# Attention kernel: each sum of values issued as two halves of the queries, with a score tile between the halves in TensorE's order

## The reference, cut to what matters

```python
qkv = x @ W_qkv + b_qkv                       # x: 16 x 1024 x 256, layer-normalised
q, k, v = jnp.split(qkv, 3, axis=2)           # 16 heads of 16 features
energy = jnp.einsum('bqhe,bkhe->bqhk', q, k)
attn = jax.nn.softmax(energy, axis=-1) / sqrt(E)
out = jnp.einsum('bihv,bvhd->bihd', attn, v)  # the sum of values
return out.reshape(B, N, E) @ W_out + b_out
```

## Time and profile before

| | us |
|---|---|
| time, median of 3 runs (3433.14 to 3438.01) | 3435.56 |
| time of the profiled execution | 3431.27 |
| its span, first to last instruction | 3429.5 |
| TensorE busy in the span | 3255.2 (95%) |
| VectorE busy | 3007.2 (88%) |
| ScalarE busy | 2703.3 (79%) |
| GpSimd busy | 1069.0 (31%) |
| first and last sum of values start at | 387.2 and 3119.8 |

### The profile page before, as it was taken

One profiled execution on the slowest core, in us unless ns is written; L12 is line 12 of the kernel. 1 busy time (PEld: TensorE's weight loads), 2 busy tenths in 40 slices (PEclk: granted clock), 3 DMA queues, 4 the chain that ended last, 5 costly groups with the idle time before them and its releaser, 6 DMA issues. The chain is left out here.

```text
span 3429.5 us, 61061 instructions
## 1 busy us (share of the span) xinstructions
PE 3255.2 (95%) x22618; PEld 1160.2 (34%) x22618; DVE 3007.2 (88%) x4484; ACT 2703.3 (79%) x5325; POOL 1069.0 (31%) x1021
## 2 busy tenths in 40 slices
PE   6998899999999999999999999999999999998997
PEld 4655222323232323232323232323232323224654
DVE  6866889999999999999999999999999998997865
ACT  5841588888888888888888888888888888887840
POOL 2440233333333232323232323232323232123410
PEclk8999799999999999999999999999999999999998
DMA  4336121313131313131313131313131312122336
GB/s 134 99 139 282 46 65 34 81 34 81 35 80 35 80 36 79 36 78 37 78 36 78 37 77 38 77 38 77 38 77 38 77 38 65 39 80 85 99 125 269
DMA packets 180619, 262.27 MB, mean 76 GB/s; under 512 B 92180, under 2 KB 132948, under 8 KB 165988
## 3 DMA queue, kind: packets, MB, share of 16 engines
q1 hardware_dynamic: 177700, 256.28, 26.9%
q10 hardware_dynamic: 2624, 2.10, 0.2%
HBM read 121.91 MB, written 51.38 MB: 51 GB/s over the span
## 5 line engine op out<-in xcount | busy, mean ns | idle before, releaser
L1706 DVE TENSOR_REDUCE attn_part_max<-attn_ps 128x2 f32<-128x1024 f32 x2048 | 2442.4, 1220 | 213.4 <-PE attn_ps L1839 178.2
L1959 ACT ACTIVATE attn_probs<-attn_ps 128x512 f32<-128x512 f32 x4096 | 2161.5, 598 | 366.6 <-PE attn_ps L1852 366.4
L1852 PE MATMUL attn_ps<-attn_q_rows,attn_k_rows 50*128 50x512 f16 x4096 | 1259.3, 384 | 43.2 <-ACT attn_probs L1959 25.2
L1839 PE MATMUL attn_ps<-attn_k_rows,attn_q_rows 48*128 48x512 f16 x4096 | 1130.5, 386 | 18.9 <-DVE attn_part_max L1706 18.2
L1852 PEld LDWEIGHTS attn_ps<-attn_q_rows,attn_k_rows 50*128 50x128 f16 x4096 | 308.0, 94 | 1329.6 <-ACT attn_probs L1959 1206.9
L1866 PE MATMUL attn_ps<-attn_probs,attn_v_even 128*32 128x512 f32 x4096 | 548.2, 607 | 0.0
L1866 PE MATMUL attn_ps<-attn_probs,attn_v_odd 128*32 128x512 f32 x4096 | 545.5, 605 | 0.7 <-ACT attn_probs L1959 0.7
L1596 POOL CAST attn_max_parts<-attn_max_whole 16x128 f16<-16x128 f32 x128 | 35.9, 280 | 1158.9 <-ACT attn_max_whole L1905 1158.8
L1839 PEld LDWEIGHTS attn_ps<-attn_k_rows,attn_q_rows 48*128 48x128 f16 x4096 | 224.3, 94 | 159.1 <-DVE attn_part_max L1706 138.6
L1800 PE MATMUL attn_ps<-attn_shared,attn_w_qk 128*128 128x256 f16 x1536 | 212.9, 276 | 1.3 <-PEq L26 1.3
L1641 POOL TENSOR_TENSOR attn_alpha_t<-attn_alpha_t 128x256 f32<-128x256 f32 x120 | 88.0, 733 | 294.5 <-ACT attn_alpha_t L1936 258.5
(11 more groups left out here) (216 smaller groups left out, 2741.4 us busy)
## 6 DMA issues: line engine op xcount, KB each, us to landing
attn_q_rows<-attn_alpha_t SPq DMA_DIRECT2D x384, 64.0 KB, 2.3
attn_k_rows<-attn_alpha_t SPq DMA_DIRECT2D x384, 64.0 KB, 2.3
ffn_x_back<-in_L_attn_x SPq DMA_DIRECT2D x16, 1024.0 KB, 13.2
after_first_ffn<-ffn_x_back SPq DMA_DIRECT2D x16, 1024.0 KB, 12.2
attn_slot_out<-attn_alpha_t SPq DMA_DIRECT2D x256, 64.0 KB, 2.3
attn_alpha_t<-inverse_denominators SPq DMA_DIRECT2D x32, 512.0 KB
attn_alpha_t<-after_first_ffn SPq DMA_DIRECT2D x16, 1024.0 KB, 9.9
after_attention<-attn_alpha_t SPq DMA_DIRECT2D x16, 1024.0 KB, 4.6
```

The lines of the kernel that those rows point to most:

```text
L1706: dve.tensor_reduce(part_max[:, G % 2, j, :, t, half], pair, AX.X, ALU.max).then_inc(dve_emptied, 1)
L1839: last = pe.matmul(ps[:, bank + e, :], q_rows[rows_e, G % NG, j, t * P:(t + 1) * P], k_rows[rows_e, G % NG, j, half * HALF:(half + 1) * HA ...
L1852: pe.matmul(ps[:, bank, :], k_rows[rows_e, G % NG, h // 2, kt * P:(kt + 1) * P], q_rows[rows_e, G % NG, h // 2, half * HALF:(half + 1) * H ...
L1959: act.activation(probs[:, quad % NQ, h, :], bank_of(s, b0), ACT.Exp, scale=1.0 / (SCALE * SCALE)).then_inc(act_emptied, 1)
```

## The change

A sum is issued as two halves: first the 256 lower queries of the window for all four heads, then the 256 upper ones. The first half stands behind score 1, ahead of the quad's second max pair; the second half stands behind score 2, where the whole sum stood. Both halves carry the wait for score 3 of the quad before. The semaphore that says that a sum is done is raised after the second half. The last sum of the program is issued as two halves in a row.

```diff
-        return ([("max", v) for v in steps[:1]] + [("score", 4 * quad)] + job + [("score", 4 * quad + 1)]
-                + [("max", v) for v in steps[1:]] + [("score", 4 * quad + 2)]
-                + [("sum", quad - 1)] * (quad > 0) + [("score", 4 * quad + 3)])
+        sums = [[("sum", 2 * (quad - 1) + i)] * (quad > 0) for i in range(2)]
+        return ([("max", v) for v in steps[:1]] + [("score", 4 * quad)] + job + [("score", 4 * quad + 1)] + sums[0]
+                + [("max", v) for v in steps[1:]] + [("score", 4 * quad + 2)] + sums[1] + [("score", 4 * quad + 3)])
...
-            def sum_values(b, b0, quad):
+            def sum_values(b, b0, n):
+
+                quad, half = divmod(n, 2)
+                columns = slice(half * 2 * P, (half + 1) * 2 * P)
                 window, kt = divmod(quad, TT)
                 G = window // CHUNKS
                 s = slot_of("score", 4 * quad + 3, b0)
                 wait(pe, act_emptied, b, lambda i: s(i) + 1)
-                if kt == 0:
+                if kt == 0 and half == 0:
...
                 for h in range(GH):
-                    last = pe.matmul(ps[32 * h:32 * h + 32, 7, :], v_ones[G // NG % 2][:, G % NG, kt, h, :], probs[:, quad % NQ, h, :],
-                                     start=(kt == 0), stop=(kt == TT - 1), skip_group_check=True)
-                last.then_inc(pv_done, 1)
+                    last = pe.matmul(ps[32 * h:32 * h + 32, 7, columns], v_ones[G // NG % 2][:, G % NG, kt, h, :], probs[:, quad % NQ, h, columns],
+                                     start=(kt == 0 and half == 0), stop=(kt == TT - 1), skip_group_check=True)
+                if half == 1:
+                    last.then_inc(pv_done, 1)
```

More of the change, by code:

```diff
@@ L1892, in _ @@
             over_batches(pe, body)
-            sum_values(B - 1, B - 1, QB * B - 1)
+            for half in range(2):
+                sum_values(B - 1, B - 1, 2 * (QB * B - 1) + half)
         @block.scalar
```

## The result

The changed kernel takes 3822.6 us (median of 4 runs, 3817.02 to 3824.08) against 3436.35 before (4 runs): 1.1126 times, 95% interval 1.1112 to 1.114. It is slower by 386 us, where 408 was forecast (3843 us).

The account below looks back on a forecast made before the run. It took the loop through ScalarE (2.39 us) to bound quads without a job and TensorE's own work (2.88) those with one; 200 + 208 = 408 us over 3431.3, plus 4 for the median, gave 3843, range 3690 to 3905.

Parts of the forecast that it names:

- The bound: Quads without a job: loop of score 3, exponential, score 2, sum, 2.39 us; with a job TensorE never waits, 2.88.
- The half at 0.57: Each half of the sum on TensorE was to take 0.57 us, two halves 1.14, against 1.00 whole.
- the part that does not shrink: In each half sum, a fixed time of about 0.14 us that does not fall with the columns.
- Quads without a job, +0.37, 200 us: The 540 quads without a job were to go from 2.39 to 2.76 us each, 200 us in all.
- The gate at 1.07: Without a job, the first half waits for score 3's exponential until 1.07 us after score 3 starts, not 0.78.
- Quads with a job, +0.43, 208 us: In 484 quads with a job, score 1 to score 3 was to go from 1.58 to 2.01 us.
- The sum: 200 us without a job plus 208 with one were to add 408 us, giving 3843 us, 1.12 times.
- rival 1: In quads without a job the first half fills TensorE's wait, gate open at 0.78: +0.08 each, 3686 us; 4 in 100.
- What costs nothing: ScalarE, VectorE, window-end copies, job banks, GpSimd and DMA queues were to add no time; last sum +0.14 once.
- The waits of ScalarE and VectorE: ScalarE's waits for scores and VectorE's for max pairs were each to grow by some 400 us.
- Overlap of sets: Within a half, sets of matmuls were to overlap while they drain, as in the whole sum, giving 0.57 us.

Follow-up runs that it names:

- e2: The kernel before with the whole sum, in its old place, taken of the quad two back instead of one back: 3433.28 us, 0.9993 times the kernel before.
- e3: The changed kernel with both halves taken of the quad two back instead of one back: 3652.68 us, 1.0635 times the kernel before.
- e1: The changed kernel with both halves back to back behind score 2, where the whole sum stood: 3440.92 us, 1.0020 times the kernel before.
- e7: The changed kernel with parts of 128 and 384 queries in place of 256 and 256: 3824.29 us, 1.1126 times the kernel before.
- e4: The changed kernel with first half behind score 2, second behind score 3, window-end copy behind score 3's exponential: 3647.17 us, 1.0623 times the kernel before.
- e6: The kernel before with the whole sum moved behind score 1 and the copy ahead of score 2's exponential: 3885.27 us, 1.1302 times the kernel before.

## Why the prediction was right

- **The bound.** The loop score 3, exponential, score 2, sum, at 2.39, holds where VectorE has nothing to reduce (the last quads), and a lag that loosens only the sum's own wait changes nothing (e2). A lag that loosens the first half's wait gives back some 170 us (e3).
- **The half at 0.57.** Traced 0.57. The reasoning from float32 rows of other shapes held. The number was right, but the part that does not shrink was given to the half, and it belongs to the visit (e1, e7): back to back, two halves cost 1.00, not 1.14. That this made no difference is luck of the case: here the halves are always parted. For e1 the prediction's 0.14 a quad would have given 143 us, and it took 6.
- **Quads without a job, +0.37, 200 us.** Traced 2.75, +0.36, which would be 194 us in 540 quads; all of them together grew by 179. The gate at 1.07 and the max pair and score 2 queued behind it are in the timeline. The rest is in quads that were not at 2.39 before or have no max pair. The eleventh quad of each sequence, where VectorE's reciprocal of 0.93 had delayed a max pair, went from 2.66 to 2.75 only (15 quads, 4 us less). The last 13, without max pairs, grew by 2.1 us together (3 us less), and one early quad with a long wait shrank from 9.3 to 3.9 (6 us less). Some 2 us are not placed.
- **Quads with a job, +0.43, 208 us.** Traced +0.41 to +0.42 with a job alone and +0.46 where it carries a transpose, 202 us together. Of the 0.41, 0.23 is the slot of the max pair, which used to run beside scores, and the rest the second entry and exit; in these quads that division is read from the timeline. The quads without max pairs put the max pair at 0.22 where there is no job.
- **The sum.** So 408 forecast, 381 in the quads, 5 outside them. No large errors cancel: both sums are a little high. The recorded range goes down to 3690 and was to take in rival 1, which by its own sum is at 3686; the measured time is far from either.
- **What costs nothing.** No wait of VectorE or of the max pairs' banks became a gate: TensorE's idle time for VectorE ahead of max pairs is 13.5 us, where it was 18.2 before. The copy at a window's end delays the gate by 0.2 in quads without a job, as before. In the 15 quads with a job behind a window's end the kernel before paid it too (3.08), and the changed kernel does not (3.29), which makes these grow by 0.21 only.
- **The step that missed.** The waits of ScalarE and VectorE were to grow by some 400 us each and grew by 278 and 303. Busy time of the exponentials grew from 2162 to 2273 and that of VectorE's reductions from 2442 to 2499, because a record that follows another at once overlaps it: four exponentials in a row take 2.06, one alone 0.60. ScalarE waits 1908 times now and 899 times before, and a thousand more breaks at 0.11 (4 x 0.60 less 2.06, for three joins) are the 111 us. The 278 and the 111 make up ScalarE's 386; for VectorE 303 and 57 leave 26 elsewhere. Idle time is no measure of the lengthening to better than that.
- **Overlap of sets.** The records of a half span 0.64 and the next instruction starts after 0.57, and in e1 sixteen records fit in 1.07: sets overlap. A span without overlap, which is how the Trainium skill's section on packing small matmuls in TensorE: Matmul & The Clock Gate could be read, does not describe this stream. Its 4 ns for each further tile of a pack is 6 to 7 ns in these traces, from one of the four matmuls of a set to the next.
- **The visit.** Between score 2 and a sum 0.31 pass where a score's slot is 0.23. Within a half the second set starts 0.24 after the first, and what follows the half starts 0.33 after the second; in e1 the sets behind the second start 0.22 apart. So entering costs about 0.1 and leaving about 0.11. e1 against the changed kernel and e3 shows that this is paid when scores stand between the halves and not when none does. It is not peculiar to float32 or to narrow outputs: a job, which is float16 like the scores but uses 128 rows, also starts 0.31 after score 0. The Trainium skill's TensorEngine Tiling (Array Packing), Key Properties, says that changing the tiling mode drains TensorE; the price at each change is in line with that. The drain itself is not seen. A rival stands beside it: after each change the first weight load is recorded together with its matmul and takes 0.09 to 0.11 (1708.01 in the changed kernel), where score 2's load behind a max pair (1708.59) is recorded 0.2 ahead of its matmul. Weights that can't be loaded ahead across a change would cost about the same, and no run separates the two.

No run beats the kernel before. With an open gate (e3, e4) a quad without a job is TensorE's own work of 2.43, and VectorE's 2.36 would not let it go far below 2.39; in quads with a job TensorE has no wait that a split could fill. Where neither limit stands, in the last quads, the split with a lag does win.

## What to carry to other kernels

Before a block of matmuls is split to let something through, read what the split meets: each further visit to matmuls of another shape (in and out again) costs about 0.2 us here, whatever the sizes, and instructions that ran side by side may lose their neighbour (0.23 a quad). Then ask whether the part that is moved forward is ready there: a piece that carries the old wait does not fill the idle time in front of that wait, it becomes what waits, and everything behind it is serialised. Summing the quad two back, whose input is ready, took that wait away (e3), but a ready piece wins only where the engine has room left, as in the last quads of e3, so read the other limits too. Follow every user of a shared ring past the move, jobs as well as scores; the one that I left out in e6 cost some 0.4 us in each quad with a job.

## What the runs showed of the hardware that was not expected

Halving a float32 matmul of 512 moving columns costs nothing by itself: four times 256 columns behind one another in the same mode took the same 1.00 us as twice 512 (1.0020 times for the whole kernel, e1), and eight more records a quad showed no limit of their own. Unequal parts of 128 and 384 columns cost the same as equal ones to 0.01 us (e7). Going from the scores to the sum and back costs about 0.2 us each time, and a max pair that used to run beside scores, or under a wait, costs 0.22 to 0.23 us when it stands by itself.
